# Attention with layer norm and a routed mixture of experts on one core: a third row buffer, another order of transposes and routing steps in six places, and the row statistics of one token group moved from VectorE to ScalarE

## The chip, the cores and the metric

The kernel runs on one core of one Trainium2 chip. The metric is the time of one execution in device microseconds (us), as the median of several runs; lower is better.

## The reference, cut to what matters

```python
# x: (2, 2048, 256); W_qk, W_v: (256, 256); Wr: (256, 8); W1: (8, 256, 1024); W2: (8, 1024, 256)
xn = layernorm(x)                                   # over the last axis, eps 1e-5
# causal attention, one head, ALiBi slope
s = softmax(mask((xn @ W_qk) @ xn.T / 16 + (kpos - qpos) * slope)) @ (xn @ W_v.T)
# mixture of 8 experts, top 1, capacity 512 tokens for each expert, in order of the tokens
p = softmax(xn @ Wr); e = argmax(p); rank = tokens before this one with the same e; keep = rank < 512
ffn = p[e] * keep * (relu(xn @ W1[e]) @ W2[e])
out = x + s * silu(ffn)
```

## The kernel before, in words

**Precision.** Products are made of float16 halves: each operand is a high half and a low half (the rest), and a product is three matmuls (high·high, high·low, low·high; `product`, lines 1419 to 1421). So every transposed or copied operand needs a "high" by ScalarE and a "low" by VectorE: `high` (L1285) and `low` (L1033) for the probabilities.

**Stages.** The 4096 tokens are 32 tiles of 128 rows, in 8 groups of 4 tiles; groups 0 to 3 are batch 0, 4 to 7 batch 1. Tiles 0 to 27 of the attention come first (`REST` is 28), then the eight experts (TensorE: `up`, `down`), then tiles 28 to 31, whose rows of the output are finished on the chip. The 28 tiles are each one pass of `tile(t)` in every engine's program; all orders are written out by hand.

**A tile t.** It has `chunks(t)` chunks of keys (1 to 4, 512 keys each, the last one shorter). In pass t the engines work on three tiles at once, step c by step c: TensorE makes the scores of tile t+1 (`score`), the product of the probabilities of tile t-1 with the values (`values`, L1510 to L1513, 0.11 us of pitch each), and transposes the probabilities of tile t (`turn`, L1491) where that is TensorE's. VectorE reads each score chunk (L1012), which frees its PSUM bank: there are two, so TensorE may start a chunk of scores only when the chunk two before it has been read. When all chunks are read, the row minimum is there (L1019) and ScalarE takes the exponentials of tile t+1 (`probs`, L1269).

**Transposes of probabilities.** Where `by_dma(t, c)` is false, TensorE transposes the chunk through PSUM (four transposes of 128x128). Where it is true, ScalarE and VectorE write the two halves into a row buffer `p_rows` (two of them, in turn) and SP issues a DMA transpose (`chunk_turn`, L552). That is so in tiles 8 to 14, 24 to 26 and 28 to 30 for some chunks and for chunk 1 of tile 15. `high` waits until the DMA of two chunks earlier has emptied its buffer; `values` waits until its own has landed.

**Groups.** Beside the tiles, each group g is normed, split in halves, turned (SP, `turn`, four DMA transposes, L509), and goes through units on TensorE: QRY twice (queries), VAL to VAL+3 (values and router logits), RANK (counts of the tokens before). PICK is VectorE's choice of the expert (L991 to L1003, with an exponential by ScalarE, L1242). `units_after(t, c)` says which of them stand behind step c of pass t. RANK's counts (L982) let POOL work out the slots (L709 to L728) and scatter the rows to the experts' slots by four indirect DMAs (L765). Only when those of group 7 have landed may SP fetch the first expert's rows (`next_rows(0)`, L544 and L545), for which TensorE's first `up` waits (L1419 with xeT).

**Row statistics.** For group 3 VectorE takes them in pass 4 (`STATS_TILE`): four `bn_stats` (L856), four `bn_aggr` (L865), one addition (L867). For two tiles of group 1 ScalarE does it at the start: `mean` (L1321) and `square` (L1327), each an activation with an accumulator output.

**Expert weights.** VectorE takes the largest magnitudes of expert 0's weights; the last piece is in pass 11 (L1062). SP writes them out and fetches them back spread over the partitions (`spread(0)`, L497 and L499), and VectorE waits for that in pass 12 (`scale`, L1073).

**SP's queue** is in order: for each t its `chunk_turn`s, then loads and stores of groups, then `turn(n)` for a group whose split is due, then `spread(0)` at t = 11, and at t = 26 `next_rows(0)` and `next_rows(1)`.

## Time and profile before

| | |
|---|---|
| median of 3 runs | 440.42 us (439.35 to 440.53) |
| profiled execution, its own time | 441.75 us |
| its span, first to last instruction | 440.0 us |
| TensorE (PE) busy | 420.4 us, 96% |
| VectorE (DVE), ScalarE (ACT), GpSimd (POOL) busy | 322.4, 222.7, 228.3 us |
| granted TensorE clock | 1.0 of full speed throughout |

A profile row of a timeline gives the start in us from the span's start, the duration, the engine, the line, what is written and read, how many were merged, and in brackets the idle time of the engine just before and what ended it. "SPq" is SP's queue: the row tells when the DMAs were issued. The passes of tiles 0 to 27 fill the span up to 219 us, the experts up to 398 us, tiles 28 to 31 the rest.

### The profile page before, as it was taken

The numbers are of one execution on the slowest core, as the hardware profiler recorded it, in microseconds if no ns is written. First come the engines' busy times: TensorE is split into PE (matmuls) and PEld (weight loads), VectorE is DVE, ScalarE is ACT, GpSimd is POOL, SyncE is SP. The second block draws the span as 40 slices with busy tenths as digits, with TensorE's granted clock in tenths as the row PEclk, the third lists the DMA queues.
The fourth block names the chain that finished last, engine by engine and source line by source line (L and its number), as shares of the span: only waits on it lengthen the run. The fifth ranks groups of instructions, "written<-read, shape, count | busy, mean of one in ns | idle before, by whom it ended". The sixth has DMA issues, their size and how long they took to land.

```text
span 440.0 us, 8367 instructions
## 1 busy us (share of the span) xinstructions
PE 420.4 (96%) x3015; PEld 288.6 (66%) x3015; DVE 322.4 (73%) x838; ACT 222.7 (51%) x444; POOL 228.3 (52%) x353
## 2 busy tenths in 40 slices
PE   6899999998999899999989999999999999999996
PEld 2667576756668676766666666666666666665666
DVE  5989778988888478778747787979796967424553
ACT  3755454452657146545424555545455545454551
POOL 3257851826544826056102566575757576757530
PEclk9999999999999999999999999999999999999999
DMA  7996898366945634266866577676888873234840
GB/s 238 294 294 151 277 295 191 74 130 163 279 90 111 139 115 117 57 216 153 120 96 232 165 245 226 205 250 176 281 156 280 179 206 98 90 120 113 159 98 31
DMA packets 104280, 76.01 MB, mean 173 GB/s; under 512 B 73263, under 2 KB 98108, under 8 KB 102192
## 3 DMA queue, kind: packets, MB, share of 16 engines
q1 hardware_dynamic: 92976, 53.11, 47.3%
q0 software_dynamic: 5824, 16.74, 12.9%
q10 hardware_dynamic: 5440, 5.64, 3.9%
q8 instruction: 24, 0.39, 0.4%
q14 instruction: 16, 0.13, 0.1%
HBM read 31.33 MB, written 28.58 MB: 136 GB/s over the span
## 4 chain that ended last, share of the span: by engine, by line
PE 64%; DVE 13%; DMA 11%; issue 4%; ACT 4%; POOL 1%; SPq 1%; another core or an unknown queue 0%; ACTq 0%; POOLq 0%; DVEq 0%
PE bank L1419 18%; PE bank L1421 18%; PE bank L1420 17%; DMA xg<-in_x 4%; DMA pT<-p_rows 3%; PE bank L1510 3%; DVE sc L1012 3%; PE bank L1513 3%; PE bank L1512 3%; PE bank L1491 2%; ACT sc L1269 2%; DVE p_rows L1033 2%; DMA rows<-xg 1%; DMA slots<-xnr,slot_idx 1%; DMA xeT<-slots 1%
## 5 line engine op out<-in xcount | busy, mean ns | idle before, releaser
L1510 PE MATMUL bank<-v_h,pT 128*128 128x257 f16 x272 | 74.7, 274 | 3.2 <-DMA pT<-p_rows 3.2
L1513 PE MATMUL bank<-v_h,pT 128*128 128x257 f16 x272 | 74.1, 272 | 0.0
L1512 PE MATMUL bank<-v_l,pT 128*128 128x256 f16 x272 | 73.7, 271 | 0.0
L1296 ACT ACTIVATE hid_h<-bank 128x512 f16<-128x512 f32 x64 | 38.1, 596 | 67.7 <-PE bank L1421 59.8
L1102 DVE SCALAR_TENSOR_TENSOR hid_l<-bank,hid_h 128x512 f16<-128x512 f32 x64 | 44.0, 688 | 38.0 <-ACT hid_h L1296 33.7
L1421 PE MATMUL bank<-w_h,hid_l 128*128 128x256 f16 x256 | 69.8, 273 | 0.0
L1419 PE MATMUL bank<-w_h,hid_h 128*128 128x256 f16 x256 | 69.8, 273 | 0.0
L1420 PE MATMUL bank<-w_l,hid_h 128*128 128x256 f16 x256 | 69.8, 273 | 0.0
L1012 DVE CUSTOM_DVE_ANT_0 sc<-bank,bias,score_mul 128x512 f32<-128x512 f32 (+2 forms) x80 | 52.9, 664 | 9.1 <-PE bank L1421 9.0
L1419 PE MATMUL bank<-xT,qT_h 128*128 128x512 f16 (+3 forms) x160 | 55.0, 347 | 3.1 <-DVE cmin L1012 1.7
L1285 ACT ACTIVATE pT<-bank 128x512 f16<-128x512 f32 (+3 forms) x50 | 24.6, 494 | 60.3 <-PE bank L1491 50.9
L1420 PE MATMUL bank<-xT,qT_h 128*128 128x512 f16 (+3 forms) x160 | 55.1, 347 | 0.0
L1421 PE MATMUL bank<-xT,qT_l 128*128 128x512 f16 (+3 forms) x160 | 55.1, 347 | 0.0
L1269 ACT ACTIVATE sc<-sc,rmin 128x512 f32<-128x512 f32 (+2 forms) x72 | 44.0, 663 | 15.5 <-DVE rmin L1019 13.3
L1419 PE MATMUL bank<-xeT,w_h 128*128 128x512 f16 x128 | 48.6, 379 | 1.8 <-DMA xeT<-slots 1.8
L1420 PE MATMUL bank<-xeT,w_h 128*128 128x512 f16 x128 | 48.5, 379 | 0.0
L1421 PE MATMUL bank<-xeT,w_l 128*128 128x512 f16 x128 | 48.5, 379 | 0.0
L1510 PEld LDWEIGHTS bank<-v_h,pT 128*128 128x128 f16 x272 | 26.4, 97 | 14.1 <-DMA pT<-p_rows 4.6
L1033 DVE SCALAR_TENSOR_TENSOR pT<-bank,pT 128x512 f16<-128x512 f32 (+3 forms) x50 | 27.9, 559 | 10.0 <-ACT pT L1285 8.7
L1512 PEld LDWEIGHTS bank<-v_l,pT 128*128 128x128 f16 x272 | 26.8, 98 | 8.6
L1290 ACT ACTIVATE w_h<-raw,wup 128x512 f16<-128x512 f32 x40 | 27.8, 716 | 9.0 <-DVE ymul L1078 9.0
L1084 DVE SCALAR_TENSOR_TENSOR w_l<-raw,wup,w_h 128x512 f16<-128x512 f32 x40 | 29.3, 749 | 3.6 <-ACT w_h L1290 2.7
(198 smaller groups left out, 919.9 us busy)
## 6 DMA issues: line engine op xcount, KB each, us to landing
raw<-in_w_e SPq DMA_DIRECT2D x5, 2048.0 KB
sc<-in_w_e SPq DMA_DIRECT2D x3, 2048.0 KB
slots<-empty ACTq DMA_DIRECT2D x1, 4224.0 KB, 18.7
gates<-gate SPq DMA_DIRECT2D x8, 512.0 KB
out<-xg SPq DMA_DIRECT2D x7, 512.0 KB
rows<-xg SPq DMA_DIRECT2D x7, 512.0 KB, 7.2
rows<-so SPq DMA_DIRECT2D x7, 512.0 KB
xg<-in_x SPq DMA_DIRECT2D x6, 512.0 KB, 4.4
```

Source lines behind the costliest of these rows:

```text
L1012: last = v.tensor_tensor_reduce(sc[:, k, c * GTOK:c * GTOK + w], score_bank(t, n)[:, 0:w], bias[:, lo:lo + w], score_mul[:, 0:1], 3e38, AL ...
L1033: v.scalar_tensor_tensor(lo, in_blocks(p), P_UP, hi, ALU.mult, ALU.subtract).then_inc(pT_lo, 1)
L1084: v.scalar_tensor_tensor(w_l[k][:, m, cols], buf[:, m, cols], wup[k][:, m:m + 1], w_h[k][:, m, cols], ALU.mult, ALU.subtract).then_inc(w_l ...
L1102: v.scalar_tensor_tensor(hid_l[:, f % HB, :], sc_ps[f % 2][:, :], 0.0, hid_h[:, f % HB, :], ALU.max, ALU.subtract).then_inc(h_lo, 1)
L1269: a_.activation(sc[:, k, cols], sc[:, k, cols], ACT.Exp, bias=least(t), scale=-1.0).then_inc(exp_made, 1)
L1296: a_.activation(hid_h[:, f % HB, :], sc_ps[f % 2][:, :], ACT.Relu).then_inc(h_hi, 1)
L1419: pe.matmul(ps, a_h, b_h, start=first, stop=False, skip_group_check=shared)
L1420: pe.matmul(ps, a_h, b_l, start=False, stop=False, skip_group_check=shared)
L1421: return pe.matmul(ps, a_l, b_h, start=False, stop=last, skip_group_check=shared)
L1510: pe.matmul(pv_ps[t % 2][:, 0:D + 1], p_h, v_h[:, at, q, 0:D + 1], start=kb == 0, stop=False)
L1512: pe.matmul(pv_ps[t % 2][:, 0:D], p_h, v_l[:, at, q, :], start=False, stop=False)
L1513: last = pe.matmul(pv_ps[t % 2][:, 0:D + 1], p_l, v_h[:, at, q, 0:D + 1], start=False, stop=kb == t % NT)
```

## The change

It adds a third row buffer (it lies in two of the four blocks of `hid_h`, which the experts use) and one landing semaphore for each parity of tile and chunk in place of two; lets TensorE turn chunk 1 of tile 15 and the DMA turn chunk 0 of tile 27; issues SP's `turn(4)` in pass 11 behind the chunks (two of its DMAs before the first half of `spread(0)`, two between the halves) where it stood at the end of pass 10; moves `next_rows(1)` behind pass 27; in tiles 23 and 24 moves group 7's VAL and VAL+1 to step 0, VAL+2 and VAL+3 to the last step of tile 23, PICK to step 0 and RANK to the last step of tile 24, and group 6's RANK from step 2 to step 1 of tile 23; in tile 31 puts each `turn` one step later; and gives the statistics of group 3 to ScalarE in passes 4 (tile 0) and 5 (tiles 1 to 3).

```diff
-        p_rows = [sb(f"p_rows{k}", [P, GT, 2, P], F16) for k in range(2)]
+        p_rows = [sb(f"p_rows{k}", [P, GT, 2, P], F16) for k in range(NX - 1)]
+        p_rows += [hid_h[:, HB - 2:HB, :].rearrange("p f t -> p (f t)").rearrange("p (b h t) -> p b h t", b=GT, h=2)]
...
             if t in (REST - 1, TILES - 1):
-                return False
+                return c == 0 and t == REST - 1
             if chunks(t) == 4:
-                return c == 1 if t == NT - 1 else c in ((1, 2) if t < NT else (0, 1, 2))
+                return t != NT - 1 and c in ((1, 2) if t < NT else (0, 1, 2))
...
-                mine = [PICK] * first + [RANK] * (last and g != NG + 1)
+                mine = [PICK] * first + [RANK] * (c == 1 if g == LATE - 1 else last and g != NG + 1)
...
-                   REST - 5: [VAL, VAL + 1] * last,
-                   REST - 4: [VAL + 2, VAL + 3] * first + [PICK] * (c == 1),
-                   REST - 3: [RANK] * first,
+                   REST - 5: [VAL, VAL + 1] * first + [VAL + 2, VAL + 3] * last,
+                   REST - 4: [PICK] * first + [RANK] * last,
...
-        STATS_TILE = {4: 3, 8: 4, 11: 5, 13: 6, 14: 7}
+        ROOT_TILES = {(4, 1): [0], (5, 0): [1, 2, 3]}
+        STATS_TILE = {8: 4, 11: 5, 13: 6, 14: 7}
...
                 for n in (*SPLIT_TILE, LATE):
-                    if t == {5: 14, LATE: REST - 8}.get(n, SPLIT_TILE.get(n)):
+                    if n != NG and t == {5: 14, LATE: REST - 8}.get(n, SPLIT_TILE.get(n)):
                         turn(n)
                 if t == FIRST_SCALE - 1:
-                    spread(0)
+                    turn(NG, range(2))
+                    top_out(0)
+                    turn(NG, range(2, GT))
+                    top_in(0)
...
                     next_rows(0)
-                    next_rows(1)
-
-            spread(1)
+            next_rows(1)
+
+            top_out(1)
+            top_in(1)
...
             def inverse(g):
-                pool.wait_ge(var_made, var_to(g))
+                if g == 3:
+                    pool.wait_ge(square3_made, GT)
+                    step(g_.tensor_scalar(var[1][:, :], mv[1][:, :, 1], 1.0 / D, EPS, ALU.mult, ALU.add))
+                    settle()
+                else:
+                    pool.wait_ge(var_made, var_to(g))
...
             def high(t, c):
...
-                    i = dma_no(t, c)
                     act.wait_ge(exp_made, n + 1)
-                    if i >= 2:
-                        act.wait_ge(pT_in[i % 2], i // 2 * 16)
+                    if dma_no(t, c) >= NX:
+                        b, m = in_rows[dma_no(t, c) - NX]
+                        act.wait_ge(pT_in[b % 2][m], landed(b, m))
...
+            def statistics(j):
+                act.wait_ge(x_in[1], 32)
+                act.wait_ge(xn_made, made_to(1))
+                act.wait_ge(square3_made, j)
+                a_.activation(unread[:, :], xg[1][:, j, :], ACT.Copy, scale=1.0 / D, accum_out=mv[1][:, j, 0:1]
+                              ).then_inc(mean3_made, 1)
+                act.wait_ge(mean3_made, j + 1)
+                a_.activation(unread[:, :], xg[1][:, j, :], ACT.Square, bias=mv[1][:, j, 0:1], scale=-1.0,
+                              accum_out=mv[1][:, j, 1:2]).then_inc(square3_made, 1)
...
                         high(t, c)
+                    for q in ROOT_TILES.get((t, c), ()):
+                        statistics(q)
...
-                    if c < chunks(t) and not by_dma(t, c):
-                        turn(t, c)
+                    k = c - 1 if t == TILES - 1 else c
+                    if 0 <= k < chunks(t) and not by_dma(t, k):
+                        turn(t, k)
...
+            turn(TILES - 1, chunks(TILES - 1) - 1)
             for c in range(chunks(TILES - 1)):
                 values(TILES - 1, c)
```

## Rows read from the trace of the kernel before

**Rows 1.** The page: busy time by engine, and the chain that ended last by engine.

```profile
PE 420.4 (96%) x3015; PEld 288.6 (66%) x3015; DVE 322.4 (73%) x838; ACT 222.7 (51%) x444; POOL 228.3 (52%) x353
...
PE 64%; DVE 13%; DMA 11%; issue 4%; ACT 4%; POOL 1%; SPq 1%; another core or an unknown queue 0%; ACTq 0%; POOLq 0%; DVEq 0%
```

**Rows 2.** Timeline of passes 4 to 6: ScalarE, VectorE and TensorE.

```profile
40.16 1.13 ACT L1269 ACTIVATE sc<-sc,rmin 128x512 f32<-128x512 f32 x2 [0.90 <-DVE rmin L1019]
...
41.39 0.60 PE L1491 MATMUL bank<-ident,sc 128*128 128x128 f32 x4
...
42.03 0.60 ACT L1285 ACTIVATE pT<-bank 128x512 f16<-128x512 f32 x1 [0.47 <-issue]
...
42.27 1.37 DVE L856 BATCH_NORM_STATS2 stats<-xg 128x6 f32<-128x256 f32 x4
...
44.16 0.75 DVE L1012 CUSTOM_DVE_ANT_0 sc<-bank,bias,score_mul 128x512 f32<-128x512 f32 x1
...
44.98 0.39 PE L1419 MATMUL bank<-xT,qT_h 128*128 128x512 f16 x1 [1.28 <-issue]
...
46.28 1.23 ACT L1269 ACTIVATE sc<-sc,rmin 128x512 f32<-128x512 f32 x2 [0.73 <-issue]
...
47.61 0.60 PE L1491 MATMUL bank<-ident,sc 128*128 128x128 f32 x4
...
48.04 0.38 PE L1419 MATMUL bank<-xT,wqk_h 128*128 128x512 f16 x1
```

**Rows 3.** Timeline of ScalarE at the start: a mean and square pair, a table load.

```profile
8.62 0.40 ACT L1321 ACTIVATE so<-xg 128x256 f32<-128x256 f32 x1
...
9.56 0.19 ACT L1327 ACTIVATION_READ_ACCUMULATOR so<-xg,mv 128x1 f32 x1
...
15.86 1.28 ACT L1346 ACT_TABLE_LOAD   x1
```

**Rows 4.** Timeline of SP's queue, passes 10 to 12.

```profile
92.00 5.12 SPq L509 DMA_TRANSPOSE xT<-xnr  x4
97.22 2.62 SPq L552 DMA_TRANSPOSE pT<-p_rows  x2
99.90 0.57 SPq L497 DMA_DIRECT2D tops<-wmax  x1
103.10 0.33 SPq L499 DMA_DIRECT2D gate<-tops  x1
```

**Rows 5.** Timelines of TensorE and VectorE, passes 12 to 14.

```profile
100.48 0.28 PE L1510 MATMUL bank<-v_h,pT 128*128 128x257 f16 x1 [1.82 <-DMA pT<-p_rows]
...
107.64 0.41 DVE L1073 TENSOR_REDUCE wtop<-gate 128x2 f32<-128x256 f32 x1
...
114.72 0.69 DVE L1033 SCALAR_TENSOR_TENSOR pT<-bank,pT 128x512 f16<-128x512 f32 x1 [0.78 <-ACT pT L1285]
...
131.14 0.39 PE L1419 MATMUL bank<-xT,qT_h 128*128 128x512 f16 x1 [0.64 <-DVE cmin L1012]
```

**Rows 6.** Timeline of TensorE, pass 16.

```profile
145.52 0.28 PE L1510 MATMUL bank<-v_h,pT 128*128 128x257 f16 x1 [1.35 <-DMA pT<-p_rows]
```

**Rows 7.** Timelines of TensorE, POOL and SP, pass 23 to the first expert.

```profile
189.01 0.29 PE L1419 MATMUL bank<-wvr_h,xT 128*128 128x264 f16 x1 [0.78 <-DVE counts L982]
...
200.95 0.25 POOL L709 TENSOR_TENSOR place<-counts,taken 128x32 f32<-128x32 f32 x1 [1.80 <-DVE counts L982]
...
216.15 2.75 SPq L545 DMA_TRANSPOSE xeT<-slots  x1
...
221.11 0.38 PE L1419 MATMUL bank<-xeT,w_h 128*128 128x512 f16 x1 [1.84 <-DMA xeT<-slots]
```

**Rows 8.** Timelines of ScalarE and TensorE, passes 28 to 31.

```profile
404.66 0.63 ACT L1285 ACTIVATE p_rows<-sc 128x512 f16<-128x512 f32 x1 [2.86 <-DMA pT<-p_rows]
...
406.48 0.39 PE L1419 MATMUL bank<-xT,qT_h 128*128 128x512 f16 x1 [0.26 <-DVE cmin L1012]
...
425.79 0.66 PE L1491 MATMUL bank<-ident,sc 128*128 128x128 f32 x4 [0.92 <-ACT sc L1269]
```

More of the change, by code:

```diff
@@ L226, in layer_kernel @@
         seed_sqv = sb("seed_sqv", [P, GT])
+        unread = sb("unread", [P, D], F16)
         bank = [ctx.enter_context(nc.psum_tensor(f"bank{k}", [P, 512], F32)) for k in range(8)]
@@ L280, in layer_kernel @@
         square_made = sem("square_made")
+        mean3_made = sem("mean3_made")
+        square3_made = sem("square3_made")
         xT_hi = sem("xT_hi")
@@ L303, in layer_kernel @@
         pT_lo = sem("pT_lo")
-        pT_in = [sem(f"pT_in{k}") for k in range(2)]
+        pT_in = [[sem(f"pT_in{k}_{c}") for c in range(NG)] for k in range(2)]
         pv_full = sem("pv_full")
@@ L374, in dma_no, with landed @@
             return chunk_no(t, c) - turn_no(t, c)
+        in_rows = [(t, c) for t in range(TILES) for c in range(chunks(t)) if by_dma(t, c)]
+        def landed(t, c):
+            return sum(by_dma(k, c) for k in range(t % 2, t + 1, 2)) * 16
         def chunk_cols(t, c):
@@ L385, in row_halves @@
         def row_halves(t, c):
-            k = dma_no(t, c) % 2
+            k = dma_no(t, c) % NX
             return p_rows[k][:, :, 0, :], p_rows[k][:, :, 1, :]
@@ L457, in var_to @@
         def var_to(g):
-            return 1 if g == 0 else g + 2
+            return 1 if g == 0 else g + 2 if g < 3 else g + 1
         def tile_rows(g, h):
@@ L492, in _, with top_out, top_in, turn @@
                          ).then_inc(slope_in, 16)
-            def spread(e):
+            def top_out(e):
                 sp.wait_ge(w_maxed, e + 1)
                 sp.dma_start(tops[e, 0:2 * P].rearrange("(p m) -> p m", m=2), wmax[:, :]).then_inc(w_put, 16)
+            def top_in(e):
                 sp.wait_ge(w_put, e * 16 + 16)
                 sp.dma_start(wall[:, :], tops[e, 0:2 * P].partition_broadcast(P)).then_inc(w_spread, 16)
-            def turn(g):
+            def turn(g, tiles=range(GT)):
                 at = key_slot(g // NG, g % NG)
@@ L506, in turn @@
                     sp.wait_ge(score_full, chunk_no(NT, 0))
-                for j in range(GT):
+                for j in tiles:
                     sp.wait_ge(xn_lo, rows_to(g))
@@ L547, in chunk_turn @@
             def chunk_turn(t, c):
-                i = dma_no(t, c)
+                k = dma_no(t, c) % NX
                 sp.wait_ge(pT_lo, chunk_no(t, c) + 1)
@@ L552, in chunk_turn @@
                 sp.dma_start_transpose(pT[:, t % 2, c * GT:c * GT + GT, :, :].rearrange("p b h t -> p (b h) t"),
-                                       p_rows[i % 2][:, :, :, :].rearrange("p b h t -> p (b h t)")
-                                       ).then_inc(pT_in[i % 2], 16)
+                                       p_rows[k][:, :, :, :].rearrange("p b h t -> p (b h t)")
+                                       ).then_inc(pT_in[t % 2][c], 16)
             def next_weights(e):
@@ L1274, in high @@
                 if by_dma(t, c):
-                    i = dma_no(t, c)
                     act.wait_ge(exp_made, n + 1)
-                    if i >= 2:
-                        act.wait_ge(pT_in[i % 2], i // 2 * 16)
+                    if dma_no(t, c) >= NX:
+                        b, m = in_rows[dma_no(t, c) - NX]
+                        act.wait_ge(pT_in[b % 2][m], landed(b, m))
                     hi, _ = row_halves(t, c)
@@ L1496, in values @@
                 if by_dma(t, c):
-                    i = dma_no(t, c)
-                    pe.wait_ge(pT_in[i % 2], i // 2 * 16 + 16)
+                    pe.wait_ge(pT_in[t % 2][c], landed(t, c))
                 else:
```

## The prediction, made before the changed kernel was timed

> **What bounds the kernel now.** I read the page first. TensorE is busy 96% of the span and holds 64% of the chain that ended last [rows 1], so no engine can be made much faster to any use; what is to be had is the time in which TensorE stands still. I therefore took TensorE's timeline, looked for every row with idle time in brackets, and for each asked the view of waits and the other engines' timelines who came late. Eight such holes lie where the change touches the code: 1.28 us ahead of pass 6 [rows 2], 1.82 in pass 12 and 0.64 in pass 14 [rows 5], 1.35 in pass 16 [rows 6], 0.78 in pass 23 and 1.84 ahead of the first expert [rows 7], 0.26 and 0.92 in passes 29 and 31 [rows 8]. A hole costs a little more than its bracket: four transposes print 0.60 us but the next matmul starts 0.43 after them [rows 2], so the printed end of the work before the hole is 0.17 too late. With 0.17 added to each the eight make 10.25 us. That is the most that could go. The rest of the work is to see who is late next.
>
> **Statistics of group 3.** VectorE reaches the scores of tile 6 (L1012) at 44.16, behind four bn_stats that start at 42.27; TensorE waits for that read until 44.98 [rows 2]. Without the statistics the read ends at about 43.0, before TensorE is there (43.70), and the hole of 1.45 closes. But ScalarE now has the work. A pair of mean and square runs from 8.62 to 9.75 [rows 3]; with the marks between them I take 1.18 us a pair. One pair in pass 4 starts at 39.2 and ends at 40.4; the exponentials of tile 5, at 40.16 before, come 0.25 later, and TensorE, which wants them at 41.39 [rows 2] when the first ends at about 41.1, does not feel it. Three pairs in pass 5 start when the high half at 42.03 is done, 42.6, and end at 46.1. Behind them stand a high half of 128x256 (0.39) and then the exponentials of tile 6, 0.65 each: the first ends at about 47.1, where before it ended at 46.9 to 47.0 (46.28 on). So TensorE's transposes of tile 6, at 47.61 before [rows 2], start at about 47.1: the change wins 0.5, not 1.45, since ScalarE is late next. Ends: a pair at 1.0 to 1.5 us gives a gain of 1.0 to a loss of 0.4. POOL gets its variance some 0.8 later and has one more small operation; the split of group 3 that waits for it had 2.5 us to spare, so I cost it at nothing.
>
> **SP's turn(4) behind the chunks of pass 11.** Before, its four transposes hold SP from 92.00 to 97.12, and both chunks of tile 11 stand behind them at 97.22 [rows 4] though the first was ready at 93.8; TensorE pays 1.82 + 0.17 for it at 100.48 [rows 5]. After, that chunk goes out at about 93.9, the second at 96.5, and TensorE starts at 98.5. But VectorE sets the end of the next passes. It was not late at 100.48, its own queue is full until 102.5, and in pass 12 it waits for the weights' magnitudes. These go out at 100.4 instead of 99.90 behind two transposes (1.28 each, a quarter of the 5.12 [rows 4]), landed 3.2 us later before (99.90 to 103.10), come back behind two more transposes at 103.6, and land about 4.0 later: 107.6, which is where VectorE took them before (107.64 [rows 5]). So VectorE wins nothing up to there, and afterwards only the 0.78 that it stood waiting for the high half of tile 13 [rows 5], which comes from TensorE's earlier transposes, and some 0.2 of others. In pass 14 TensorE is caught by VectorE again (0.64 at 131.14 [rows 5], which stays). I take a gain of 1.0; ends: 0, if the magnitudes come back 1 us later than I say, and 2.0, if VectorE is no bound.
>
> **Tile 15.** Chunk 1 was turned by DMA and TensorE waited 1.35 + 0.17 = 1.52 for it at 145.52 [rows 6]. Four transposes on TensorE cost 0.43. They find their bank read and the exponentials done. Gain 1.1; ends 0.5 (a transpose waits for VectorE's low half in pass 15) and 1.1. The passes behind it have no hole up to 189.01.
>
> **Tiles 23 and 24.** TensorE waited 0.95 for VectorE's copy of group 6's counts [rows 7], since the second of group 7's value units needed its bank. With two value units ahead of RANK and two behind, the copy is wanted later; VectorE gets to it about 0.65 later, as two units of 0.68 stand in front on TensorE. I expect a hole of 0.2. POOL idled 1.80 before it could begin group 7's slots at 200.95 [rows 7]; RANK of group 7 now stands at the end of pass 24, some 3 us earlier, so POOL begins as soon as group 6's scatter is issued, which is 0.65 later than before: 1.80 - 0.65 = 1.15 earlier. From there to the fetch of the expert's rows all is in series (slots, four scatters, their landing, SP, 216.15 [rows 7]), so the first `up` starts 1.15 earlier, at 219.96 on the old clock. TensorE itself gets there 0.75 + 0.43 (the transposes of chunk 27,0 that it no longer does) earlier, and so still waits some 2 us: **these two gains are not added, the scatter is the bound.** 1.15 in all; ends 0.5 and 1.8.
>
> **Chunk 0 of tile 27 by DMA.** Its transpose stands in SP's queue behind `next_rows(0)`, which waits for the scatter. So it is issued at 217.8 (2.75 us behind 215.0 [rows 7]), and a chunk takes 3.2 to 4.5 from issue to use (401.4 to 404.66 in pass 28 [rows 8]; 141.02 to 145.52 in pass 16 [rows 6]): it lands at 221.0 to 222.3, and TensorE wants it one `up` (1.3 us) after 219.96, at 221.3. A loss of 0 to 1.0, which I put at 0.4. The trace shows no such pair in the queue. The Trainium skill (DMA: Bandwidth & Descriptors, section Queues, rings and completion order) says that descriptors of one ring are consumed in order; by that alone the loss would be nearer its upper end, and the sum 0.6 smaller. `next_rows(1)` moves behind it and feeds an expert that starts 20 us later: nothing.
>
> **Tiles 28 to 31.** With a third buffer ScalarE's third high half no longer waits 2.86 us for a DMA (404.66 [rows 8]; it is so in three passes, 28, 29 and 30). VectorE then reads the last scores of tile 29 some 2 us earlier, and TensorE's hole of 0.26 + 0.17 at 406.48 goes. Its hole of 0.92 + 0.17 ahead of tile 31's transposes (425.79 [rows 8]) is the same delay once more, and would close by the buffer alone; the later place of the transposes makes it sure, and costs nothing, since three chunks of values stand between the last transpose and its use. Gain 1.5; ends 1.0 and 1.7.
>
> **The sum.** 0.5 + 1.0 + 1.1 + 1.15 - 0.4 + 1.5 = 4.85 us. The profiled execution took 441.75 us, 440.0 of it span; it becomes 436.9. That execution is 1.33 above the median; off the median of 440.42 the same 4.85 gives **435.6 us**.
>
> **Rivals.**
> - *Half of it only.* Where data comes back through memory the clock does not move: the magnitudes land later than 107.6 and group 6's later counts eat the scatter's gain. For it: both are waits of which the trace shows the latency once or twice; against it: each has a row above. Then 0.5 + 0 + 1.1 + 0.2 - 0.7 + 1.5 = 2.6, so 437.8 us.
> - *The holes all close.* VectorE and ScalarE are no bound behind the holes: 10.25 less the 0.81 of pass 14, which stays, and less 2.0 that the scatter still holds ahead of the expert: 7.4, so 433.0 us (the 0.43 that pass 15 pays, pass 27 gets back). Against it: ScalarE's row at 46.28.
> - *It does not do what it says.* Each wait is passed on to the next engine in line, as 2 us of hole ahead of the expert stay in my own sum: 440.2 us. Against it: the last hole stands so near the end that nothing is left to take its place.
> - *Slower, by table loads.* Square may lie in another function table than the exponentials. No row shows a square beside an exponential; in the start both ran without a load after the square root's [rows 3]. Then pass 4 and pass 5 need two loads each, 1.28 us and 0.03 of gap a load [rows 3]. The exponential of tile 5 ends at 43.8 against 41.39 wanted, 2.4 late; that of tile 6 at 47.1 + 2.4 + 2.6 = 52.1 against 47.61, 4.5 late instead of 0.5 early. 435.6 + 5.0 = 440.6, and with pairs of 1.3 us 441.0. It decides as soon as a load costs more than 1.25. The Trainium skill (ScalarE: Activation LUTs, Rules for kernel authors) budgets about 2.7 us for every switch to another set; by that figure, against 1.28 in this trace, the same rival would end at about 446.
>
> **How the numbers follow.** What a measurement of this kernel can tell from no change is about 0.3%, 1.3 us. My case (a gain of 3.2 to 6.5) gets 0.60, half of it 0.18, all of it 0.07, nothing 0.09, slower 0.06. The range must leave out the last two and may leave a little more: the low end is the third case, 433.0; the high end adds up the poor ends that go together (0 + 0 + 0.5 + 0.5 - 1.0 + 1.5 = 1.5, 438.9), so 438.8. Faster by over 0.3%: 0.60 + 0.18 + 0.07, and a bit of the half case falls short: 0.84. Within 0.3%: 0.10. Slower: 0.06.
>
> **What would show it.** Pass 6: the matmul of rows 2 without a bracket, a bracket of some 0.8 before the transposes of tile 6, and ScalarE without idle time from 42 to 47. Pass 12: no bracket at L1510, VectorE at L1073 with a bracket instead. Pass 16: no wait for p_rows. POOL without its 1.80 before L709. Ahead of the first `up` a bracket of about 2 still, and perhaps one at the values of tile 27. ScalarE's three waits for p_rows gone, and none ahead of tile 31's transposes. I am wrong if the page shows more table loads than six, if the first bracket of pass 6 only moves, or if the expert starts no earlier than the passes before it allow.

## The result, and the profile after

The changed kernel takes 436.87 us in the median of 5 runs (436.09 to 437.49), the kernel before 440.42 on the same chip: a ratio of 0.9925, 95% interval 0.9905 to 0.9946, so 3.3 us faster (2.4 to 4.2). The prediction was 435.6, its range 433.0 to 438.8. The profiled execution took 436.17 us, its span 434.4 against 440.0: 5.6 less, which is more than the medians differ by. A second pair of profiles (e10 and e11, below) shows where most of the surplus comes from.

The page after, in the lines of [rows 1]:

```profile
PE 420.3 (97%) x3015; PEld 288.6 (66%) x3015; DVE 324.4 (75%) x829; ACT 224.8 (52%) x460; POOL 229.3 (53%) x354
...
PE 81%; DVE 9%; DMA 4%; ACT 3%; SPq 2%; issue 2%; ACTq 0%; another core or an unknown queue 0%; DVEq 0%
```

TensorE's work is the same, and it now holds 81% of the chain instead of 64%; DMA's share fell from 11% to 4%. ScalarE has the 8 activations and 8 accumulator reads of the statistics more, and as many table loads as before, six.

Passes 5 and 6 after, timelines of ScalarE, VectorE, TensorE and POOL (answers to [rows 2]):

```profile
42.34 0.41 ACT L1383 ACTIVATE unread<-xg 128x256 f16<-128x256 f32 x1
...
43.59 0.42 ACT L1383 ACTIVATE unread<-xg 128x256 f16<-128x256 f32 x1
...
46.40 0.38 ACT L1309 ACTIVATE pT<-bank 128x256 f16<-128x256 f32 x1 [0.41 <-remote]
46.68 1.22 ACT L1293 ACTIVATE sc<-sc,rmin 128x512 f32<-128x512 f32 x2
...
44.17 0.62 DVE L1036 CUSTOM_DVE_ANT_0 sc<-bank,bias,score_mul 128x384 f32<-128x384 f32 x1 [0.77 <-PE bank L1458]
...
46.49 0.20 DVE L1006 COPY counts<-bank 128x40 f32<-128x40 f32 x1 [1.50 <-remote]
...
43.38 0.38 PE L1456 MATMUL bank<-xT,qT_h 128*128 128x512 f16 x1
...
47.45 0.66 PE L1528 MATMUL bank<-ident,sc 128*128 128x128 f32 x4 [1.29 <-ACT sc L1293]
```

The bracket ahead of pass 6 is gone (43.38 instead of 44.98), a pair takes 1.25, and 1.29 stand ahead of tile 6's transposes instead. They start at 47.45, before at 47.61: most of the hole only moved. Two rows are odd. VectorE copies RANK's counts at 46.49, after 1.50 idle, 3 us after those matmuls ended (43.52), and ScalarE idles 0.41 for transposes that ended at 43.33. (`<-remote` is printed where the profile names no engine of this core as what ended the wait.) I call such a row a late mark: a mark is the semaphore signal by which one engine tells another that its work is done.

Passes 12 to 14 after, SP's queue, VectorE and TensorE ([rows 4, 5]):

```profile
97.56 2.58 SPq L522 DMA_TRANSPOSE xT<-xnr  x2
100.18 0.58 SPq L507 DMA_DIRECT2D tops<-wmax  x1
100.81 2.50 SPq L522 DMA_TRANSPOSE xT<-xnr  x2
103.36 0.58 SPq L512 DMA_DIRECT2D gate<-tops  x1
...
111.25 0.37 SPq L543 DMA_DIRECT2D xg<-in_x  x1
...
107.35 0.42 DVE L1097 TENSOR_REDUCE wtop<-gate 128x2 f32<-128x256 f32 x1 [1.83 <-DMA gate<-tops]
...
115.52 0.75 DVE L880 BATCH_NORM_STATS2 stats<-xg 128x6 f32<-128x256 f32 x2 [0.95 <-DMA xg<-in_x]
...
98.28 0.27 PE L1546 MATMUL bank<-v_h,pT 128*128 128x257 f16 x1
...
117.79 0.34 PE L1456 MATMUL bank<-xT,qT_h 128*128 128x384 f16 x1 [0.70 <-issue]
121.32 0.39 PE L1456 MATMUL bank<-xT,qT_h 128*128 128x512 f16 x1 [0.48 <-DVE cmin L1036]
127.61 0.39 PE L1456 MATMUL bank<-xT,qT_h 128*128 128x512 f16 x1 [0.44 <-DVE cmin L1036]
```

The values of chunk 0 of tile 11 (98.28) wait no more. VectorE now stands 1.83 for the magnitudes in pass 12 and 0.95 for the rows of a later group in pass 13, where the kernel before has no wait for the magnitudes and 0.21 for the rows. TensorE stands three times in passes 13 and 14, where it stood once in pass 14. The profile puts two of the three down to VectorE and names nothing for the one at 117.79; the same row in e6, at 116.98, is put down to VectorE (`cmin`, L1036) too.

Pass 23 to the first expert after, TensorE, POOL and SP ([rows 7]):

```profile
187.35 0.29 PE L1456 MATMUL bank<-wvr_h,xT 128*128 128x264 f16 x1
...
196.77 0.24 POOL L733 TENSOR_TENSOR place<-counts,taken 128x32 f32<-128x32 f32 x1
...
205.73 0.97 POOL L789 DMA_INDIRECT slots<-xnr,slot_idx  x1 [0.30 <-issue]
...
209.00 0.37 SPq L557 DMA_DIRECT2D enote<-slots  x1
209.42 2.20 SPq L558 DMA_TRANSPOSE xeT<-slots  x1
213.83 1.23 SPq L565 DMA_TRANSPOSE pT<-hid_h  x1
...
215.60 0.38 PE L1456 MATMUL bank<-xeT,w_h 128*128 128x512 f16 x1
```

POOL starts group 7's slots without the idle 1.80, SP fetches the expert's rows at 209.42 instead of 216.15, and the first `up` has no bracket. I had expected 2 us to stay there. In passes 28 to 31 ScalarE's waits for `p_rows` are gone ([rows 8]); the transposes of tile 31 have no bracket.

The start of a pass (us), by TensorE's timeline. Columns: the first pair, the second pair (e10, e11), and the eight experiments e1 to e8; "first up" is TensorE's first matmul of expert 0, "last matmul" the start of its last one.

| | before | after | e10 before | e11 after | e1 | e2 | e3 | e4 | e5 | e6 | e7 | e8 |
|---|---|---|---|---|---|---|---|---|---|---|---|---|
| 7 | 54.27 | 54.16 | 54.08 | 54.41 | 54.14 | 53.70 | 53.77 | 53.65 | 53.74 | 53.60 | 53.79 | 53.63 |
| 11 | 87.79 | 87.75 | 87.39 | 87.89 | 87.36 | 86.93 | 86.99 | 86.88 | 86.96 | 86.82 | 87.10 | 86.86 |
| 15 | 134.79 | 133.97 | 134.23 | 134.99 | 134.00 | 132.74 | 133.36 | 133.35 | 133.55 | 133.39 | 133.49 | 131.12 |
| 17 | 152.08 | 149.86 | 151.52 | 150.87 | 149.89 | 148.63 | 151.28 | 149.23 | 149.44 | 149.28 | 149.37 | 147.01 |
| 23 | 181.07 | 178.77 | 180.43 | 179.78 | 178.80 | 177.54 | 180.19 | 178.14 | 178.35 | 178.18 | 178.28 | 175.92 |
| 27 | 214.10 | 211.09 | 213.38 | 212.40 | 211.12 | 209.87 | 212.51 | 211.05 | 210.67 | 210.51 | 210.61 | 208.25 |
| first up | 221.11 | 215.60 | 218.33 | 216.91 | 215.63 | 214.38 | 217.02 | 215.56 | 215.18 | 215.46 | 215.12 | 212.76 |
| 28 | 398.20 | 393.50 | 395.42 | 394.10 | 393.59 | 391.56 | 394.20 | 392.75 | 392.45 | 392.55 | 392.29 | 389.95 |
| last matmul | 436.40 | 430.86 | 433.50 | 430.99 | 430.62 | 428.57 | 431.10 | 429.78 | 430.56 | 429.45 | 429.33 | 426.85 |

A stretch that an edit doesn't touch repeats within 0.1 us as a rule (17 to 23 takes 28.90 to 28.99 in all twelve), so a part can be priced by its own stretch far better than by the whole time. There are exceptions: from the first `up` to pass 28 it takes 177.1 to 177.3 in ten of them, but 177.90 in after and 177.96 in e1, and 7 to 11 takes 33.2 to 33.6.

### The profile page after: what moved, and what is told of

The parts are those of the page before. It is cut to its first block, busy times and chain, and to the rows that moved or that the text cites. A ratio compares the mean times of both kernels' runs of the same rounds, so it can differ in the third digit from the quotient of the medians.

```text
span 434.4 us, 8377 instructions
## 1 busy us (share of the span) xinstructions
PE 420.3 (97%) x3015; PEld 288.6 (66%) x3015; DVE 324.4 (75%) x829; ACT 224.8 (52%) x460; POOL 229.3 (53%) x354
## 4 chain that ended last, share of the span: by engine, by line
PE 81%; DVE 9%; DMA 4%; ACT 3%; SPq 2%; issue 2%; ACTq 0%; another core or an unknown queue 0%; DVEq 0%
PE bank L1456 20%; PE bank L1458 20%; PE bank L1457 20%; PE bank L1546 6%; PE bank L1549 6%; PE bank L1548 6%; PE bank L1528 3%; DMA xg<-in_x 2%; DVE sc L1036 2%; DMA rows<-xg 2%; SPq L522 1%; DVE w_l L1108 1%; DVE p_rows L1057 1%; DVE stats L880 1%; ACT sc L1293 1%
## 5 line engine op out<-in xcount | busy, mean ns | idle before, releaser
L1036 DVE CUSTOM_DVE_ANT_0 sc<-bank,bias,score_mul 128x512 f32<-128x512 f32 (+2 forms) x80 | 52.9, 663 | 13.5 <-PE bank L1458 13.2
```

Source lines behind the costliest of these rows:

```text
L1036: last = v.tensor_tensor_reduce(sc[:, k, c * GTOK:c * GTOK + w], score_bank(t, n)[:, 0:w], bias[:, lo:lo + w], score_mul[:, 0:1], 3e38, AL ...
```

## The experiments

**e1 to e4, one part undone each, on one chip.** Before took 438.94 us there.

```diff
e1
-        ROOT_TILES = {(4, 1): [0], (5, 0): [1, 2, 3]}
-        STATS_TILE = {8: 4, 11: 5, 13: 6, 14: 7}
+        ROOT_TILES = {}
+        STATS_TILE = {4: 3, 8: 4, 11: 5, 13: 6, 14: 7}
...
e2
-                    if n != NG and t == {5: 14, LATE: REST - 8}.get(n, SPLIT_TILE.get(n)):
+                    if t == {5: 14, LATE: REST - 8}.get(n, SPLIT_TILE.get(n)):
...
-                    turn(NG, range(2))
                     top_out(0)
-                    turn(NG, range(2, GT))
                     top_in(0)
e3
-                return t != NT - 1 and c in ((1, 2) if t < NT else (0, 1, 2))
+                return c == 1 if t == NT - 1 else c in ((1, 2) if t < NT else (0, 1, 2))
e4
-                mine = [PICK] * first + [RANK] * (c == 1 if g == LATE - 1 else last and g != NG + 1)
-                REST - 5: [VAL, VAL + 1] * first + [VAL + 2, VAL + 3] * last,
-                REST - 4: [PICK] * first + [RANK] * last,
+                mine = [PICK] * first + [RANK] * (last and g != NG + 1)
+                REST - 5: [VAL, VAL + 1] * last,
+                REST - 4: [VAL + 2, VAL + 3] * first + [PICK] * (c == 1),
+                REST - 3: [RANK] * first,
```

> The changed kernel with one part undone: the statistics of group 3 are taken by VectorE in tile 4 again. Theory A, from the trace after: the part moved the hole from ahead of pass 6 (1.28 us in brackets) to ahead of the transposes of tile 6 (1.45 start to start) and won nothing, because the marks of TensorE's work in pass 5 come late whoever takes the statistics. Then this kernel is within 0.4 us of the changed one, 436.9, ratio to the kernel before 0.992 to 0.994, the hole ahead of pass 6 is back at about 1.3 and the one ahead of tile 6's transposes is gone. Theory B, my prediction's: ScalarE's share wins 0.5 us and up to 1.4, so this kernel takes 437.4 to 438.3, ratio 0.994 to 0.996.

435.43 us, ratio 0.9909 (0.9886 to 0.9933). Pass 7 starts at 54.14, in e2 to e4 on the same chip at 53.65 to 53.77: ScalarE's share of the statistics is worth 0.4 to 0.5 us. Theory A, read off the first pair alone, falls by this stretch; the prediction's 0.5 stands on this chip. The whole time cannot decide it: 435.43 lies under what either theory said.

> The changed kernel with one part undone: the four transposes of group 4 stand ahead of the chunks of tile 11 in SP's queue again, and the weights' magnitudes go out and come back in one piece. Theory A: the part wins only what VectorE does not hold back in passes 13 and 14, 0.5 to 1.0 us at the start of pass 15; the hole of 1.8 to 2.0 comes back in pass 12 at the values of chunk 0 of tile 11, the holes of 0.86, 0.65 and 0.61 in passes 13 and 14 shrink to 0.3 to 0.8 in all. 437.4 to 437.9, ratio 0.994 to 0.996. Theory B: VectorE's row of work is the same and sets the start of pass 15 alone, 0 to 0.2 us, 436.9 to 437.1. Theory C: the whole 2.0 is lost again, 438.9.

434.45 us, ratio 0.9901 (0.9878 to 0.9925). Timelines of SP, VectorE and TensorE in e2:

```profile
98.73 0.57 SPq L507 DMA_DIRECT2D tops<-wmax  x1
101.85 0.33 SPq L512 DMA_DIRECT2D gate<-tops  x1
...
106.47 0.41 DVE L1094 TENSOR_REDUCE wtop<-gate 128x2 f32<-128x256 f32 x1
...
99.30 0.28 PE L1543 MATMUL bank<-v_h,pT 128*128 128x257 f16 x1 [1.81 <-DMA pT<-p_rows]
```

The hole in pass 12 is back, yet passes 11 to 14 take 45.81 us, and 46.37, 46.47 and 46.64 in e3, e4 and e1. **With this part undone they are 0.6 to 0.8 us faster**, which none of the three theories allowed. VectorE takes the magnitudes without a wait; in the changed order it stands 2.0 to 2.8 for them in e1, e3 and e4, and 0.6 to 1.1 more in pass 13 for the rows of a later group, whose load SP issues at 109.00 in e2 and at 110.57 in e3. Passes 13 and 14 give back more than the 1.98 that pass 12 won.

The old order is not the whole of the difference to the kernel before: that one has the same order and takes 46.84 (e10) and 47.00 us for passes 11 to 14, a whole us more than e2. Its VectorE waits for rows in passes 13 and 14 (0.27 and 0.43 in e10), e2's does not. No run isolates which of the other parts removes that.

> The changed kernel with one part undone: chunk 1 of tile 15 is turned by DMA again. Theory A: the hole in pass 16 at the values of that chunk is back with 1.3 to 1.6 us, TensorE saves 0.43 of transposes, and nothing between there and the first expert has slack to take the 1.1 up, now that the scatter no longer sets the start of the expert: 438.0, ratio 0.995. Theory B: the rows of the tokens' scatter still set the start of the expert, so 1.1 us in pass 16 is swallowed there: 436.9, ratio 0.992.

437.38 us, ratio 0.9963 (0.9938 to 0.9988). SP and TensorE in e3:

```profile
139.58 1.23 SPq L565 DMA_TRANSPOSE pT<-hid_h  x1
141.09 4.60 SPq L522 DMA_TRANSPOSE xT<-xnr  x3
...
144.71 0.28 PE L1546 MATMUL bank<-v_h,pT 128*128 128x257 f16 x1 [1.99 <-DMA pT<-hid_h]
```

Passes 15 and 16 take 17.92 us against 15.88 in e4: 2.0, as the chunk is used 5.1 us after its issue here. In the kernel before it was 4.5 [rows 6], and the same stretch shows 17.29 against 15.88 between e10 and e11: 1.4. Nothing behind it takes the 2.0 up: from pass 17 to the first `up` it takes 65.74, as in e1. Theory A, and more of it.

> The changed kernel with one part undone: value units, choice and ranks of group 7 stand where they stood before (tiles 23, 24 and the start of 25). Theory A: the part was worth 3 us or more, not 1.15: the ranks of group 7 come 3 us later, its four scatters begin 1.8 to 4 us later, meet the DMA transposes of tile 26 and land 4 to 5.5 us after issue instead of 3.3, and a hole of 1.5 to 2.5 us opens ahead of the first up; with the hole of 0.95 in pass 23 the whole costs 2.5 to 3.5 us: 439.4 to 440.4, ratio 0.998 to 1.0. Theory B, my prediction's sum: 1.15 us, 438.0, ratio 0.995, the scatter landing 5.5 us after its issue in both orders.

436.3 us, ratio 0.9937 (0.9917 to 0.9958). TensorE, POOL and SP in e4:

```profile
185.96 0.29 PE L1457 MATMUL bank<-wvr_h,xT 128*128 128x264 f16 x1 [0.66 <-DVE counts L1007]
...
197.27 0.25 POOL L734 TENSOR_TENSOR place<-counts,taken 128x32 f32<-128x32 f32 x1 [1.16 <-DVE counts L1007]
...
206.09 0.98 POOL L790 DMA_INDIRECT slots<-xnr,slot_idx  x1 [0.31 <-issue]
...
208.85 0.37 SPq L558 DMA_DIRECT2D enote<-slots  x1
```

Both theories fall. The stretch from pass 23 to 27 is 0.6 longer (32.91 against 32.32), no hole stands ahead of the first `up`, and SP goes on 2.8 us after the last scatter's issue. So neither the 5.6 us of the kernel before (210.17 to 215.73) nor its hole of 1.84 comes with this order. So a second profile of the kernel before was needed.

**e5 to e8, on another chip.** Before took 438.76 us there.

```diff
e5
-            k = dma_no(t, c) % NX
+            k = dma_no(t, c) % 2
e6
-                return c == 0 and t == REST - 1
+                return False
e7
-                for j in range(GT):
+                for j in range(GT if g else 0):
                     g_.indirect_dma_start(
e8
-        FIRST_MAX, FIRST_SCALE, FIRST_SPLIT = (9, 9, 9, 9, 10, 10, 10, 11), 12, (13, 13, 13, 14, 15, 20, 21, 22)
+        FIRST_MAX, FIRST_SCALE, FIRST_SPLIT = (9, 9, 9, 9, 10, 10, 10, 11), 12, (16, 16, 17, 18, 20, 21, 21, 22)
```

(e5 also sets the waits for two buffers, e7 the counts for the scatters left out.)

> The changed kernel with the third buffer for halves that are turned by DMA taken away again; the later place of tile 31's transposes stays. Theory A: ScalarE's third high half waits again in passes 28, 29 and 30, VectorE reads the last scores of tile 29 later, and TensorE stands 0.3 to 0.5 us at the start of pass 29 or in it; the late transposes of tile 31 keep the hole of 0.92 ahead of them shut. 0.4 to 0.8 us, 437.3 to 437.7, ratio 0.993 to 0.995. Theory B, by my prediction: the buffer alone carries nearly all of the term, 1.4 us, 438.3. Theory C: nothing, the late transposes carry all, 436.9.

436.56 us, ratio 0.9966 (0.9944 to 0.9987). ScalarE and TensorE in e5:

```profile
407.82 0.63 ACT L1309 ACTIVATE p_rows<-sc 128x512 f16<-128x512 f32 x1 [3.15 <-DMA pT<-p_rows]
...
400.72 0.39 PE L1456 MATMUL bank<-xT,qT_h 128*128 128x512 f16 x1 [0.24 <-DVE cmin L1036]
...
421.48 0.28 PE L1546 MATMUL bank<-v_h,pT 128*128 128x257 f16 x1 [0.61 <-DMA pT<-p_rows]
```

From pass 28 to the last matmul it takes 38.11 us, as before does (38.08 in e10), against 36.90 to 37.04 in e6 to e8. Without the buffer the whole of the term, 1.1 to 1.2 us, is gone: the late transposes of tile 31 win nothing alone, they only move the wait to the values behind them (421.48). Whether the buffer would win all of it with the transposes in their old place was not run. Between A and B, nearer B.

> The changed kernel with chunk 0 of tile 27 turned by TensorE again. Theory A, from the trace after, in which no hole stands ahead of the first up nor at the values of that chunk: TensorE does four more transposes of 0.11 us and starts the expert 0.43 later: 437.3, ratio 0.9935. Theory B, my prediction's: the DMA turn behind the fetch of the rows costs TensorE 0.4 and this kernel is as fast or up to 0.5 faster: 436.4 to 436.9, ratio at or under 0.9925.

435.43 us, ratio 0.9926 (0.9905 to 0.9947). From the start of pass 27 to the first `up` it takes 4.95 us, as in e10, against 4.51 in every profile with the chunk turned by DMA: 0.44, theory A.

> The changed kernel without the four scatters of group 0's rows to their slots (40.5 to 45.6 us in the trace after); the rest of the program is the same, and the rows of 512 tokens are missing from the experts' input. It asks why marks of TensorE's work come 1.4 to 3.0 us late in pass 5. Theory A: marks of every engine are held up while POOL issues the scatters: without them no mark in pass 5 comes later than 0.3 us, the high half of chunk 1 of tile 5 starts within 0.1 us of the end of the last square, the exponentials of tile 6 start 0.4 to 0.5 us earlier, and the hole ahead of tile 6's transposes shrinks from 1.45 to about 1.0. Theory B: the four transposes by DMA on SP's queue in the same stretch do it, and the marks are late all the same. Time 436.4 to 436.9 by A, 436.9 by B: the trace decides, not the time.

435.24 us (n = 4), ratio 0.9919 (0.9893 to 0.9946). The copy of the counts comes 0.54 us after their matmuls, but in e6, with the scatters, it comes after 0.53, and neither has a late mark. So this run tells nothing of the cause. ScalarE, VectorE and TensorE in e6:

```profile
45.85 0.36 ACT L1309 ACTIVATE pT<-bank 128x256 f16<-128x256 f32 x1
...
44.01 0.19 DVE L1006 COPY counts<-bank 128x40 f32<-128x40 f32 x1
...
46.88 0.66 PE L1528 MATMUL bank<-ident,sc 128*128 128x128 f32 x4 [0.77 <-ACT sc L1293]
```

> The changed kernel with the eight splits of the first expert's weights moved from tiles 13, 13, 13, 14, 15, 20, 21, 22 to tiles 16, 16, 17, 18, 20, 21, 21, 22. Theory A: VectorE is what holds TensorE in passes 13 and 14 (holes of 0.86, 0.65 and 0.61), each split is 0.75 us of it, and VectorE has 0.8 to 3.8 us free in each of the passes that take them: 1.5 to 2.1 us faster, 434.8 to 435.4, ratio 0.9875 to 0.989. Theory B: the holes close, and the marks of the chunks turned by DMA or the scatter ahead of the expert are late next: under 0.7 us, ratio over 0.991.

433.96 us, ratio 0.9894 (0.9872 to 0.9915). Of the holes in passes 13 and 14 one of 0.25 (in brackets, at 116.32) is left; pass 15 starts 2.3 to 2.4 earlier than in e5 to e7, and the last matmul starts 2.5 earlier than in e7 and 2.6 earlier than in e6, 0.44 of which is e6's own loss. Theory A in kind: VectorE bound these passes, and in the profiles what it is relieved of arrives at the end in full. The medians show less, 1.3 and 1.5 to e7 and e6; the profiled execution of e8, at 432.16, was its fastest, 1.8 under its median.

**e9 to e11, on a third chip.** Before took 440.28 us there. e10 and e11 are the two kernels of the case, unchanged. (e9 also puts group 4's four transposes in one piece behind the chunks.)

```diff
e9
-        FIRST_MAX, FIRST_SCALE, FIRST_SPLIT = (9, 9, 9, 9, 10, 10, 10, 11), 12, (13, 13, 13, 14, 15, 20, 21, 22)
+        FIRST_MAX, FIRST_SCALE, FIRST_SPLIT = (9, 9, 9, 9, 9, 10, 10, 10), 12, (16, 16, 17, 18, 20, 21, 21, 22)
-        ROOT_TILES = {(4, 1): [0], (5, 0): [1, 2, 3]}
+        ROOT_TILES = {(4, 1): [0], (5, 0): [1, 2], (5, 1): [3]}
...
+                    if (t, c) == (FIRST_SCALE - 1, 0):
+                        top_out(0)
                     if by_dma(t, c):
                         chunk_turn(t, c)
+                    if (t, c) == (FIRST_SCALE - 1, 0):
+                        top_in(0)
...
+                    if (t, c) == (5, 1):
+                        probs(6, range(2))
                     if c < chunks(t):
                         high(t, c)
```

> The changed kernel with three edits for VectorE and ScalarE. One: the eighth piece of the magnitudes' maximum moves from tile 11 to tile 10, and the magnitudes go out ahead of chunk 0 of tile 11 and come back behind it, with the four transposes of group 4 in one piece behind both chunks. Two: the splits of the first expert's weights stand in tiles 16 to 22, as in the run with later splits. Three: ScalarE takes the exponentials of tile 6 ahead of the last pair of statistics and of the high half of chunk 1 of tile 5. Theory A: VectorE's wait of about 2 us for the magnitudes in tile 12 goes, the last hole of 0.41 in pass 13 closes and the 0.61 ahead of pass 12 stays, and the hole of 0.93 ahead of tile 6's transposes closes as the exponentials start 1.1 us earlier: 1.0 to 1.4 us faster than the run with later splits alone, ratio 0.985 to 0.988. Theory B: the edits only move the waits (VectorE's longer row in tiles 9 and 10 opens a hole of 0.3 to 0.7 ahead of pass 11 or 12, or the late high half stops the values of chunk 1 of tile 5): within 0.4 us of that run, ratio 0.988 to 0.990.

434.93 us, ratio 0.9897 (0.9851 to 0.9944). ScalarE, TensorE, SP and VectorE in e9:

```profile
44.65 1.21 ACT L1293 ACTIVATE sc<-sc,rmin 128x512 f32<-128x512 f32 x2
...
63.64 5.23 SPq L565 DMA_TRANSPOSE pT<-p_rows  x2
...
72.07 0.28 PE L1548 MATMUL bank<-v_h,pT 128*128 128x257 f16 x1 [1.69 <-DMA pT<-p_rows]
...
105.35 0.41 DVE L1097 TENSOR_REDUCE wtop<-gate 128x2 f32<-128x256 f32 x1
```

Each edit does its work: tile 6's transposes start at 46.01 and pass 7 at 52.67, 1.7 before e11; VectorE no longer waits for the magnitudes, and passes 12 to 14 take 34.74 us against 35.15 in e8. But the 1.7 are gone at 72.07, where a chunk sent at 63.64 is not there yet. Theory B, by another transfer than it named. One more hole, 0.70 for VectorE at 157.93, ahead of pass 20, stands in no other profile here, though e8 and e12 have the same splits; it is not explained.

> The kernel before, unchanged, with a second profile. It asks which of the rows on which the prediction rested belong to the kernel and which to that one execution. Theory A, from six profiles of kernels near the changed one, none of which has a mark later than 0.7 us after its work ahead of the experts, where the first profile of before has marks 1 to 3 us late in four places: the hole ahead of pass 6 (1.4) and those in passes 12, 14, 16 and 23 (2.0, 0.8, 1.5 to 2.2, 0.9) are there again, but the last scatter lands under 3.5 us after its issue instead of 5.5, and the hole of 1.84 ahead of the first up is gone or under 0.5. Span 437.5 to 438.5 instead of 440.0. Theory B: the landing of 5.5 and the hole ahead of the first up belong to the kernel, in the state that only all parts of the change together remove: hole of 1.5 to 2 again, span 439.5 to 440.3.

439.89 us, ratio 0.9999 (0.9969 to 1.0029), span 437.1 (theory A had said 437.5 to 438.5). POOL, SP and TensorE in e10, then POOL and SP in the first profile of before:

```profile
208.42 0.98 POOL L765 DMA_INDIRECT slots<-xnr,slot_idx  x1 [0.30 <-issue]
...
212.27 0.37 SPq L544 DMA_DIRECT2D enote<-slots  x1
...
218.33 0.38 PE L1419 MATMUL bank<-xeT,w_h 128*128 128x512 f16 x1
```

```profile
210.17 0.98 POOL L765 DMA_INDIRECT slots<-xnr,slot_idx  x1 [0.30 <-issue]
...
215.73 0.37 SPq L544 DMA_DIRECT2D enote<-slots  x1
```

The holes of passes 6, 12, 14, 16 and 23 are there again, start to start 1.41, 1.98, 0.61, 1.56 and 0.86. The one ahead of the first `up` is not, and SP goes on 3.9 us after the last scatter's issue instead of 5.6 (theory A: under 3.5). The last scatter is also issued 28.0 us after the start of pass 23, in the first profile 29.1. Theory A: that hole, 2.0 us, belonged to the first profile and not to the kernel. With one profile on each chip the record can't say whether to that execution or to that chip; the changed kernel, profiled on the same chip, does not have it.

> The changed kernel, unchanged, with a second profile, beside the kernel before on the same chip. Theory A: the late marks of its first profile (1.4 to 3.0 us in pass 5) and its hole of 0.70 in expert 6 were of that execution: the exponentials of tile 6 start at 46.1 to 46.3, the hole ahead of its transposes is 0.93 instead of 1.45, pass 7 starts at 53.6 to 53.8, the last matmul ends 1.1 to 1.3 us earlier than in the first profile; ratio 0.990 to 0.993. Theory B: they belong to the kernel and show again.

436.45 us, ratio 0.992 (0.9884 to 0.9956). ScalarE, VectorE and TensorE in e11:

```profile
46.65 0.38 ACT L1309 ACTIVATE pT<-bank 128x256 f16<-128x256 f32 x1 [0.62 <-remote]
...
46.74 0.20 DVE L1006 COPY counts<-bank 128x40 f32<-128x40 f32 x1 [2.33 <-remote]
...
47.69 0.66 PE L1528 MATMUL bank<-ident,sc 128*128 128x128 f32 x4 [1.50 <-ACT sc L1293]
```

Theory B in pass 5: the marks are late again, so this was not one execution's. Theory A in expert 6: the hole of 0.70 (at 360.60 in the first profile) is not there. It is no trait of that one execution alone, though: e1 is as slow through the experts, with a hole in brackets of 0.31 at 342.09.

**e12, on a fourth chip** (before 439.89 us): e9 with the load of the first expert's weights one pass earlier.

```diff
-                if t == 5:
+                if t == 4:
                     sp.dma_start(raw[:, :, :], w_k[0]).then_inc(w_in[1], 16)
```

> The run with three edits for VectorE and ScalarE, and one more: the load of the first expert's weights (2 MB) is issued in pass 4 instead of pass 5, about 45.5 instead of 50.1 us. Theory A: the 1.5 us won ahead of pass 7 were given back at 72.07, where chunk 0 of tile 8, issued to the DMA queue at 63.64, landed only after 8 us, since the DMA engines are still busy with that load until about 70; issued 4.6 us earlier, the load is over by about 66, the chunk lands under 6 us after its issue, and the hole of 1.86 shrinks to under 0.4: ratio 0.981 to 0.986 and pass 12 starts at 95.0 to 95.5. Theory B: the load runs into the transposes of group 2 (38.6 to 44.2) and the rows of tiles 4 to 7, and opens a hole of 1 us or more ahead of the query unit of group 2 in pass 6; or the chunk is late for the group's rows that go out ahead of it, not for the load: ratio 0.987 to 0.991.

432.98 us, ratio 0.9828 (0.9783 to 0.9874), the lowest of all. TensorE in e12:

```profile
47.30 0.38 PE L1458 MATMUL bank<-xT,wqk_h 128*128 128x512 f16 x1 [0.52 <-DMA xT<-backs]
...
71.86 0.28 PE L1548 MATMUL bank<-v_h,pT 128*128 128x257 f16 x1 [0.62 <-DMA pT<-p_rows]
```

Each theory has a row. The hole at 72 shrinks from 1.69 to 0.62 (not under 0.4), and B's hole ahead of group 2's query unit opens with 0.52. The chunk still takes 7.5 us from its issue (64.37), though the load, issued at 46.4, landed 12.1 later, so the load was not all of it. The ratio is where A put it, but pass 12 starts at 96.66, not at 95.0 to 95.5, and 96.87 in e9: by the profiles the earlier load won 0.2 there. So that it made the lower ratio is not shown; e9 and e12 were timed on different chips. e12's single profile (span 432.2) is longer than e8's (430.4), 1.5 of it behind the start of pass 28, where TensorE stands 0.41 and 0.64; the intervals of the two overlap, and which is better is open. Both have a lower ratio than the changed kernel, e12 clear of its interval; e8 shares a chip only with close relatives of it (e5 to e7), and every run of e8 is under every run of e6.

## Why the prediction was right, and where it was not

By stretch, in us gained: the prediction, before to after in the first pair of profiles and in the second (e10 to e11), and what the part is worth by its undoing on the chips of e1 to e8.

| part | predicted | first pair | e10 to e11 | undone |
|---|---|---|---|---|
| statistics (to pass 7) | 0.5 | 0.1 | -0.3 | 0.4 to 0.5 |
| untouched (7 to 10, 17 to 22, experts) | 0 | -0.8 | -0.3 | |
| turn(4) (11 to 14) | 1.0 | 0.8 | -0.3 | -0.6 to -0.8 |
| tile 15 (15, 16) | 1.1 | 1.4 | 1.4 | 2.0 |
| tiles 23, 24 (23 to 26) | 1.15, with the next row's gain in it | 0.7 | 0.3 | 0.6 |
| chunk 27,0 (27 to first up) | -0.4 | 2.5 | 0.4 | 0.4 |
| end (28 to 31) | 1.5 | 0.8 | 1.2 | 1.1 to 1.2 |
| sum, before rounding | 4.85 | 5.5 | 2.5 | about 4, without the untouched row |

The likeliest case was the right kind: the holes of the kernel before are there again in its second profile, all but the one ahead of the expert, and part of their time goes to whoever is late next. That the total came out as near as it did is partly luck. The measured 3.3 is 1.5 less than the sum; two of the six terms, turn(4) and chunk 27,0, had the wrong sign in the second pair and by undoing, and their errors go opposite ways. The stretch from 23 to the first `up` was put at 1.15 - 0.4 = 0.75 by two steps that both failed, and measures 0.3 + 0.4 in the second pair. The two pairs of profiles stand on either side of the medians, so the total rests on the medians alone. Point by point:

- **Statistics.** ScalarE was next late, as said, with a bracket of 0.77 where 0.8 was forecast (e6). The pairs took 1.25 instead of 1.18. Where marks come late the gain is 0.1 or less. By the sign that I had put down (wrong if the first bracket of pass 6 only moves) this part failed in both pairs, and held on the chips of e1 to e8. The rival of table loads fell at once: six loads of 1.28 us in both kernels, so Square ran among exponentials without one. By the Trainium skill (ScalarE: Activation LUTs, Rules for kernel authors) a switch is to be budgeted at about 2.7 us; in these runs a load takes 1.28, with 0.03 of gap around it, and there is none for this pair.
- **turn(4): the step that failed.** I wrote that the magnitudes would land where VectorE took them before, and that it would then win 0.78 and some 0.2. The first half held in the first pair (107.35 for 107.64), and there the stretch won 0.8. The second half did not hold elsewhere: the stretch lost 0.3 in the second pair, and e2, which undoes the part, is 0.6 to 0.8 faster in it. In e2, with the old order, VectorE takes them without a wait; in the new order they go out and come back behind two transposes each, and VectorE stands 1.8 to 2.8. I had named that bracket and priced it at nothing; VectorE's idle time ahead of L1073 is zero in [rows 5], so all of it is new. And I left out that the load of the next rows stands behind the same transposes (0.95 more for VectorE in pass 13).
- **Tile 15.** Right in kind; the transposes cost TensorE 0.2 where I took 0.43 (pass 15 takes 7.02 in e10, 7.24 in e11).
- **Tiles 23, 24, the scatter.** The step that failed is "the scatter is the bound". The 5.6 us from issue to SP's next step were the first profile's; it is 2.8 to 3.9 in the thirteen others, and then TensorE itself sets the start. My own side sum for that case, 0.75 + 0.43, is near what e4 and e6 measure: 0.6 + 0.44. The hole in pass 23 went to 0.24, as forecast (0.2).
- **Chunk 27,0.** The loss of 0.4 was a gain of as much: SP had issued the fetch of the rows by 211.6, so nothing stood ahead of the chunk at 213.83, and TensorE's four transposes are saved.
- **End.** The mechanism held; the term was 0.3 too large.

## What to carry to other kernels

Before a wait is moved off the engine that bounds, look at the next engine's idle time ahead of the operation that your move delays: if it has none, the move takes from it. Take a second profile before building on a single long latency; here 2 of the 10 us of holes were in one profile only. And price each edit by its own stretch of the timeline, which as a rule repeats within 0.1 us where whole runs scatter by 1 or more, and compare more than one pair: turn(4) won 0.8 in the first and lost 0.3 in the second.

## What the runs showed that I had not expected

**Late marks, perhaps of the chip.** In the first pair and in e9, e10 and e11 the counts of group 1, whose matmuls end at 43.5 to 43.7, are copied at 46.4 to 46.7 in pass 5. In before and e10 VectorE is busy for most of that time, but there ScalarE idles 2.54 and 2.48 us up to its high half of 128x256 in pass 5. ScalarE idles for such marks 0.7 to 0.8 more around 173 to 177 in all five, and ScalarE or VectorE 1.5 to 2.2 around 195 to 199 in four (not in e10). In e2 to e8 and e12 the copy comes 0.5 us after its matmuls (in e1 VectorE is still busy then), and in these nine profiles no wait over 0.3 us ends in `<-remote`. The profiles of e1 to e8 came from two chips, those of e9 to e11 from a third and that of e12 from a fourth, so it may be a property of the chip; both kernels show it. The median of before was 440.4 and 440.3 us where the marks were late and 438.9, 438.8 and 439.9 where not, too little apart to settle it. The clusters lie beside POOL's scatters (40.53 to 45.63 in the profile after), but e6 has the same scatters and prompt marks, and the run without them fell on a chip without late marks. The cause stays open.

**A DMA turn that takes 8 us.** A chunk takes 3.1 us from issue to use in pass 27 (213.83 to 216.98), 4.5 to 5.1 in pass 16 and 8.4 in pass 8 (63.64 to 72.07 in e9). The DMA engines move 91, 93 (in e3) and 219 GB/s in these stretches, so the longest stands where most else is under way; e12 shows that the load of the weights is only part of it. An earlier TensorE meets it there, so what e9 won up to pass 7 is lost again in pass 9.
